# Slice attention: the second half of an image beside the first half of the next, written out, and transposes for products with the identity

## What is computed

```
h = x @ W0 + b0
sw = jax.nn.softmax(h @ Ws + bs, axis=-1)          # 16 slices a token
qkv = (h @ Wqkv + bqkv)                            # 8 heads of 32
denom = jnp.sum(sw, axis=1)[:, None, :, None] + 1e-09
qs = jnp.einsum('bhnd,bns->bhsd', q, sw) / denom   # ks, vs likewise
attn = jax.nn.softmax(jnp.einsum('bhsd,bhtd->bhst', qs, ks) / scale, axis=-1)
tok = jnp.einsum('bhst,bhtd->bhsd', attn, vs)
out = jnp.einsum('bhsd,bns->bnhd', tok, sw).reshape(b, n, H * D)
return out @ Wout + bout                           # added to x
```

## Time and profile before

| | |
|---|---|
| median of three runs | 10232.95 us (10220.48, 10232.95 and 10233.31) |
| the profiled execution's own time | 10221.47 us |
| its span in the trace | 10219.7 us |
| busy over the span | PE 8073.3 us (79%), DVE 7633.6 (75%), POOL 6829.2 (67%), ACT 5138.6 (50%) |
| slice attention in the span | from about 9430 to 9728 us |

### The profile page before, as it was taken

One profiled execution on the slowest core, in us unless ns is written; L12 is line 12 of the kernel. 1 busy time (PEld: TensorE's weight loads), 2 busy tenths in 40 slices (PEclk: granted clock), 3 DMA queues, 4 the chain that ended last, 5 costly groups with the idle time before them and its releaser, 6 DMA issues. The chain is left out here.

```text
span 10219.7 us, 112146 instructions
## 1 busy us (share of the span) xinstructions
PE 8073.3 (79%) x34375; PEld 3937.8 (39%) x34375; DVE 7633.6 (75%) x6810; ACT 5138.6 (50%) x6133; POOL 6829.2 (67%) x3866
## 2 busy tenths in 40 slices
PE   0158888888888888888888879799749999985769
PEld 0123333333333333333333333233237777753522
DVE  8769999999999999999999953477735655534144
ACT  0046666666666666666666623367615554421123
POOL 0059999999999999999999963300067777761047
PEclk9679999999999999999999988699969999965579
DMA  0057677677767766666676740000032222210022
GB/s 10 0 138 182 175 179 180 178 178 177 180 175 178 181 177 177 180 177 177 177 181 175 178 87 1 11 1 1 1 35 29 27 29 27 27 17 5 0 71 89
DMA packets 385896, 1064.96 MB, mean 104 GB/s; under 512 B 106434, under 2 KB 129602, under 8 KB 383378
## 3 DMA queue, kind: packets, MB, share of 16 engines
q1 hardware_dynamic: 338482, 1044.16, 39.8%
q0 software_dynamic: 47136, 17.04, 3.8%
HBM read 995.98 MB, written 63.50 MB: 104 GB/s over the span
## 5 line engine op out<-in xcount | busy, mean ns | idle before, releaser
L535 POOL TENSOR_TENSOR hC<-h,Cb 128x1024 f32<-128x1024 f32 x1536 | 3600.9, 2357 | 434.6 <-DVE h L630 413.7
L630 DVE TENSOR_TENSOR_SCAN h<-dA,B_ps 128x1024 f32<-128x1024 f32 x1344 | 3073.1, 2287 | 156.4
L308 PE MATMUL y_ps<-hC,con 128*128 128x512 f32 x6144 | 2969.9, 606 | 80.5 <-DVE gz L636 80.3
L455 ACT ACTIVATE dA<-delta,negA 128x1024 f32<-128x1024 f32 x1344 | 1535.3, 1145 | 1204.6 <-DVE h L630 1200.3
L616 DVE TENSOR_TENSOR B_ps<-dx,B_ps 128x1024 f32<-128x1024 f32 x1344 | 1623.9, 1208 | 166.3 <-PE B_ps L302 166.3
L308 PEld LDWEIGHTS y_ps<-hC,con 128*128 128x128 f32 x6144 | 1186.2, 194 | 1145.5 <-issue 943.2
L2626 POOL DMA_INDIRECT g_got<-scratch_node,g_idx x1152 | 1143.6, 993 | 359.8 <-issue 350.7
L302 PE MATMUL B_ps<-Bpart,sel 96*128 96x512 bf16 x2688 | 828.6, 390 | 648.0 <-DVE h L630 645.7
L2676 PE MATMUL g_pick<-g_third,g_hot 128*128 128x256 bf16 x10752 | 1260.9, 274 | 0.0
L2676 PEld LDWEIGHTS g_pick<-g_third,g_hot 128*128 128x128 bf16 x10752 | 1020.2, 98 | 203.8 <-issue 81.9
L2722 ACT ACTIVATE g_hot<-g_fill 128x512 bf16<-128x512 f32 x896 | 485.8, 594 | 653.2 <-PE g_fill L2659 651.5
(11 more groups left out here) (493 smaller groups left out, 11652.4 us busy)
## 6 DMA issues: line engine op xcount, KB each, us to landing
Cb<-scratch_c_rows SPq DMA_DIRECT2D x3072, 256.0 KB, 4.1
drive<-scratch_c_rows SPq DMA_DIRECT2D x384, 256.0 KB, 5.2
eb_share<-scratch_gate_rows SPq DMA_DIRECT2D x128, 256.0 KB, 3.5
scratch_c_rows<-BCrow SPq DMA_DIRECT2D x96, 256.0 KB, 4.0
scratch_edge<-g_out SPq DMA_DIRECT2D x64, 384.0 KB, 2.3
par<-in_ssm SPq DMA_DIRECT2D x48, 395.5 KB, 5.3
g_got<-scratch_node,g_idx POOLq DMA_INDIRECT x1152
scratch_place<-s_zero SPq DMA_DIRECT2D x4, 1024.0 KB, 11.1
```

The costliest lines, as they stand in the source:

```text
L308: last = nc.tensor.matmul(y_ps[:, hs], con[:, K_ID:K_ID + P], hC[k % DEEP][:, hs], start=(k == 0), stop=(k == STEPS - 1))
L455: A(dA[k % DEEP][:, :], delta[d][:, :], ACT.Exp, scale=negA[:, n:n + 1]).then_inc(decay_ready, 1)
L535: G.tensor_tensor(hC[k % DEEP][:, :], hst[k % DEEP][:, :], Cb[k % DEEP][:, :], ALU.mult).then_inc(prod_ready, 1)
L630: V.tensor_tensor_scan(hst[k % DEEP][:, ::step], decayed[:, ::step], driven[:, ::step], 0.0, ALU.mult, ALU.add).then_inc(scanned, 1)
```

## The change

In `slice_attn_stage` the hardware loops are replaced by a Python loop that writes every image out. Each turn of it holds the second half of image `img` ("old") and the first half of image `img + 1` ("new"), interleaved group by group on each engine; there are nine turns, the first with only a first half and the last with only a second half. Each half has its own three semaphores. To let the halves coexist, `swT` has two buffers; the results of `attnT`, `v` and `fold` go to other columns or banks of PSUM (`psS`, `psO`, `psQ`). The copy `tw` is gone: `turn` reads `tn_sb` itself, and `turn` and `swT` are `nc.tensor.transpose` in place of a product with the identity. The two memsets of POOL count in `loaded`. Outside the stage, `EndSearch` counts its two POOL operations in one semaphore `made`, `ad0` is cleared by DVE and not by POOL, and the late store counts in `loaded`.

```diff
--- before.py
+++ after.py
@@ -1838,9 +1838,19 @@
     ALU, ACT, AX = mybir.AluOpType, mybir.ActivationFunctionType, mybir.AxisListType.X
     BLK = range(PER)
     HG = 4
-    pe_s = Steps("turn hT h logits swT pool poolT qk v scores attnT tokT fold out")
-    act_s = Steps("copy tnT hTc esw swTc poolTc qkc eat attnTc foldc")
-    dve_s = Steps("hx lg max sub sum rsum sw dn rdn pooled vc qdiag smax ssub ssum srec attn tokm tok outb t")
+
+
+    pe_a = Steps("turn hT h logits swT pool")
+    act_a = Steps("tnT hTc esw swTc")
+    dve_a = Steps("hx lg max sub sum rsum sw dn rdn pooled")
+
+
+    pe_b = Steps("poolT qk v scores attnT tokT fold out")
+    act_b = Steps("poolTc qkc eat attnTc foldc")
+    dve_b = Steps("vc qdiag smax ssub ssum srec attn tokm tok outb t")
+
+    def count(steps, name, img):
+        return steps.after(name, img) - 1
...
-        tw = sb("tw", [P, PER, C])
-        swT = sb("swT", [SLICES, L])
+        swT = [sb(f"swT{k}", [SLICES, L]) for k in range(2)]
...
-        loaded, ones_set = sem("loaded"), sem("ones")
-        pe_done, act_done, dve_done = sem("pe"), sem("act"), sem("dve")
+        ATT, FOLD = 2 * SLICES, 2 * HG * SLICES
+        loaded = sem("loaded")
+        pe_a_done, act_a_done, dve_a_done = sem("pe_a"), sem("act_a"), sem("dve_a")
+        pe_b_done, act_b_done, dve_b_done = sem("pe_b"), sem("act_b"), sem("dve_b")
...
-                nc.gpsimd.memset(hx[:, :, :], 1.0).then_inc(ones_set, 1)
-                nc.gpsimd.memset(at[:, :, :], 0.0).then_inc(ones_set, 1)
+                nc.gpsimd.memset(hx[:, :, :], 1.0).then_inc(loaded, 16)
+                nc.gpsimd.memset(at[:, :, :], 0.0).then_inc(loaded, 16)
...
-                with pe.Fori(0, B) as img:
...
-                    act("copy")
-                    for i in BLK:
-                        last = M(psM[0:C, i * P:(i + 1) * P], tw[:, i, :], ID, start=True, stop=True)
-                    done(last)
...
+                pe.wait_ge(loaded, 64)
+                for img in range(-1, B):
+                    new, old = img + 1 < B, img >= 0
+                    if old:
+                        dve_first("pooled", img)
+                        M(psS[0:C + 1, 0:SLICES], pooled[:, :], con[0:SLICES, K_ID:K_ID + SLICES], start=True, stop=True
+                          ).then_inc(pe_b_done, 1)
+                    if new:
+                        if old:
+                            act_first("swTc", img)
+                        for i in BLK:
+                            last = nc.tensor.transpose(psM[0:C, i * P:(i + 1) * P], tn_sb[:, (img + 1) * PER + i, :], ID)
+                        last.then_inc(pe_a_done, 1)
+                    if old:
+                        act_last("poolTc", img)
+                        for j in range(4):
+                            last = M(psQ[:, j * SLICES:(j + 1) * SLICES], w[0:C + 1, SW_QKV + j * P:SW_QKV + (j + 1) * P], poolT[:, :],
+                                     start=True, stop=True)
+                        last.then_inc(pe_b_done, 1)
+                        if img >= 1:
+                            dve_last("outb", img - 1)
+                        M(psO[0:SLICES, 0:HD3], poolT[:, :], w[0:C + 1, SW_QKV + 2 * HD3:SW_QKV + 3 * HD3],
+                          start=True, stop=True).then_inc(pe_b_done, 1)
+                    if new:
+                        act_first("tnT", img + 1)
+                        for hs in halves:
+                            last = M(psM[:, hs], w[0:C, SW_0:SW_0 + P], tnT[:, hs], start=True, stop=True)
+                        last.then_inc(pe_a_done, 1)
+                        if old:
+                            dve_first("hx", img)
+                        for i in BLK:
+                            last = M(psH[:, i * C:(i + 1) * C], tnT[:, i * P:(i + 1) * P], w[0:C, SW_0:SW_0 + C],
+                                     start=True, stop=True)
+                        last.then_inc(pe_a_done, 1)
+                    if old:
+                        dve_last("qdiag", img)
+                        for g in range(2):
+                            last = M(psS[0:HG * SLICES, g * SLICES:(g + 1) * SLICES], qd[:, g, :, :].rearrange("p h s -> p (h s)"),
+                                     qk[:, 2 + g, :], start=True, stop=True)
+                        last.then_inc(pe_b_done, 1)
+                    if new:
+                        act_first("hTc", img + 1)
+                        for i in BLK:
+                            last = M(psL[:, i * SLICES:(i + 1) * SLICES], hT[:, i * P:(i + 1) * P], w[0:C, SW_S:SW_S + SLICES],
+                                     start=True, stop=True)
+                        last.then_inc(pe_a_done, 1)
+                    if old:
+                        dve_last("attn", img)
+                        for g in range(2):
+                            last = M(psS[0:SLICES, ATT + g * HG * SLICES:ATT + (g + 1) * HG * SLICES], at[:, g, :],
+                                     con[:, K_ID:K_ID + HG * SLICES], start=True, stop=True)
+                        last.then_inc(pe_b_done, 1)
+                    if new:
+                        dve_first("sw", img + 1)
+                        for i in BLK:
+                            last = nc.tensor.transpose(psM[0:SLICES, i * P:(i + 1) * P], sw[:, i, :], ID)
+                        last.then_inc(pe_a_done, 1)
+                        for i in BLK:
+                            last = M(psG[0:SLICES, 0:C + 1], sw[:, i, :], hx[:, i, :], start=i == 0, stop=i == PER - 1)
+                        last.then_inc(pe_a_done, 1)
+                    if old:
+                        act_last("attnTc", img)
+                        for g in range(2):
+                            last = M(psQ[:, g * HG * SLICES:(g + 1) * HG * SLICES], v[:, g * P:(g + 1) * P],
+                                     atT[:, g * HG * SLICES:(g + 1) * HG * SLICES], start=True, stop=True)
+                        last.then_inc(pe_b_done, 1)
+                        dve_last("tok", img)
+                        for g in range(2):
+                            last = M(psQ[0:SLICES, FOLD:FOLD + C], tok[:, g, :], w[:, SW_OUT + g * C:SW_OUT + (g + 1) * C],
+                                     start=g == 0, stop=g == 1)
+                        last.then_inc(pe_b_done, 1)
+                        act_last("foldc", img)
+                        for i in BLK:
+                            last = M(psO[:, i * C:(i + 1) * C], swT[img % 2][:, i * P:(i + 1) * P], fold[:, :], start=True, stop=True)
+                        last.then_inc(pe_b_done, 1)
...
-                    act.wait_ge(dve_done, dve_s.all(img))
-                    A(tw[:, :, :], tn_sb[:, bass.ds(img * PER, PER), :], ACT.Copy).then_inc(act_done, 1)
...
+                    if old:
+                        pe_last("v", img)
+                        final(V.tensor_copy(v[:, :], psO[0:SLICES, 0:HD3]))
+                        dve.wait_ge(act_b_done, count(act_b, "qkc", img))
+                        final(V.tensor_tensor(qd[:, :, :, :], qk[:, 0:2, :].unsqueeze(2).broadcast_to([P, 2, HG, SLICES]), mask, ALU.mult))
+                    if new:
+                        pe_first("h", img + 1)
+                        first(V.tensor_tensor(hx[:, :, 0:C], psH[:, :].rearrange("p (i c) -> p i c", i=PER),
+                                              row(w[:, SR_B0:SR_B0 + C], [P, PER, C]), ALU.add))
+                    if old:
+                        pe_last("scores", img)
+                        final(V.reduce_max(rs[:, 0, :], sc, AX))
+                        own_last("smax", img)
+                        final(V.tensor_tensor(at4, sc, rs[:, 0, :].unsqueeze(2).broadcast_to(wide2), ALU.subtract))
+                    if new:
+                        pe_first("logits", img + 1)
+                        first(V.tensor_tensor(sw[:, :, :], psL[:, 0:PER * SLICES].rearrange("p (i s) -> p i s", i=PER),
+                                              row(w[:, SR_BS:SR_BS + SLICES], [P, PER, SLICES]), ALU.add))
+                        own_first("lg", img + 1)
+                        first(V.reduce_max(r8[:, 0, :], sw[:, :, :], AX))
+                        own_first("max", img + 1)
+                        first(V.tensor_tensor(sw[:, :, :], sw[:, :, :], r8[:, 0, :].unsqueeze(2).broadcast_to(wide), ALU.subtract))
+                    if old:
+                        dve.wait_ge(act_b_done, count(act_b, "eat", img))
+                        final(V.reduce_sum(rs[:, 1, :], at4, AX))
+                        own_last("ssum", img)
+                        final(V.reciprocal(rs[:, 1, :], rs[:, 1, :]))
+                        own_last("srec", img)
+                        final(V.tensor_tensor(at4, at4, rs[:, 1, :].unsqueeze(2).broadcast_to(wide2), ALU.mult))
+                    if new:
+                        dve.wait_ge(act_a_done, count(act_a, "esw", img + 1))
+                        first(V.reduce_sum(r8[:, 1, :], sw[:, :, :], AX))
+                        own_first("sum", img + 1)
```

(83 more changed lines are left out.)

192 lines of the change are left out of this document (39 added, 153 removed).

## The result

The changed kernel takes 10162.11 us, the median of four runs from 10148.26 to 10164.97. The kernel before has 10232.19 us, with 10220.48 to 10233.31. The ratio is 0.9931, with an interval of 0.9914 to 0.9949. The forecast was 10164 us. The profiled execution took 10164.08 us, its span 10162.3, with a granted clock of 0.91 on average.

The account below looks back on a forecast made before the run. Slice attention was taken as bound by one image's latency: 293.4 us would become 228 (seven turns of 27.6, ends 20.1 and 15.0), 65 us plus 2 for the clock, giving 10164 us; range 10135 to 10192.

Parts of the forecast that it names:

- The chain and its overlap: Slice attention: one image's latency bounds the stage; overlap can fill PE's idle time, some 82 us of the 293.
- The ends: Slice attention: first half alone takes 20.1 us, second half alone 15.0 us, besides seven full turns.
- The waits: PE in a full turn: three waits stay, logits to swT 2.3 us, tokT to fold 1.0, fold to out 0.5.
- The sum of a turn: Full turn of slice attention: PE's groups 23.8 us plus waits 3.8 make 27.6 us, PE busy 86%.
- The sign given for a turn: Slice attention, sign of being right: a turn repeats every 26.5 to 27.6 us.
- The clock: Slice attention: clock rises behind pool in about half the turns, 0 to 8 us, taken as 2 to 4.
- The whole time: Whole kernel: 10154.5 us against the profiled execution, 10166 by the median's step; 10164 us forecast.
- Do transposes raise the clock?: TensorE: yes, by the sort stage's trace; by the skill's rule the gain would be 65 us and not 67.
- A: Slice attention: denser stream holds 2.4 GHz, turn 16.3 us, gain 154 us, near 10079; full form 4%.
- B: Slice attention: waits taken as covered show, 3 to 5 us a turn; gain 30 to 44 us, 10189 to 10203; 10%.
- C: Written-out program stalls on instruction arrival, decisive from 8 us a turn; at 12 us a turn 10264; 3%.
- D: Whole kernel: no change within 0.2%, 20 us; needs a stall of 6 to 8 us a turn; 3%.

Follow-up runs that it names:

- serial_written_out: Changed kernel without its overlap: still written out with transposes, but each image's first half starts after the previous image's last addition; 10210.21 us, 0.9974, stage 274.3 us.
- the better order: Changed kernel with old softmax ahead of new on DVE, attnT and tokT ahead of swT, fold before pool; 10134.59 us with transposes, 10110.71 with products.
- the reordered kernels: Changed kernel with attnT and tokT ahead of swT and fold before pool, turn and swT as transposes or products, single or doubled; 10104.58 to 10137.32 us.
- turns_in_loop: Kernel before, still a loop, with transposes in turn and swT except each group's first block, which stays a product; 10230.64 us, 0.9996, stage 289.6 us.
- fold_mid_twice: Changed kernel with attnT and tokT ahead of swT, fold before pool, and transposes of turn and swT each issued twice; 10104.58 us, 0.9875, stage 180.4.
- fold_mid_products: Changed kernel with attnT and tokT ahead of swT, fold before pool, and products in turn and swT; 10110.71 us, 0.9881, stage 179.0.
- fold_mid: Changed kernel with old softmax ahead of new on DVE, attnT and tokT ahead of swT, fold before pool; 10134.59 us, 0.9908, stage 199.2.

## Why the prediction was right

**The chain and its overlap** held. PE's idle time in the one chain of an image was what the overlap filled: 51 us of the gain vanish when the halves run in sequence (`serial_written_out`). The ends were forecast at 20.1 and 15.0 and came out at 20.1 and 15.0.

**The waits** held nearly as summed: 2.1 for 2.3 (1.53 + 0.15 and two tails of 0.2, with attnT between), 1.0 (0.79 and the tail) and 0.5 (0.30 and the tail). None of those taken as covered shows in a row.

**The sum of a turn** was 27.6, and a turn without a rise takes 27.97. The missing 0.4 lie mostly in the tail of a group's last pass, which was put at some 0.2 us for every group. It is 0.2 behind turn, `h` and `out`, but only 0.07 behind the others: v is busy 1.04 and holds PE 0.96 (0.86 was summed), hT 3.44 (3.30), scores 0.54 (0.43), pool 1.85 (1.70), swT 1.80 (1.69), poolT 0.27 (0.2). HT shows that it hangs on what follows: its tail was 0.2 before logits and is 0.07 before scores. Together these six take 0.7 more, the first wait is 0.2 shorter, and turn and qk (1.71 and 1.66 for 1.74 and 1.70) take 0.07 less. Why the tail differs no run shows.

The sign given for a turn, a repeat every 26.5 to 27.6 us, was met by none of the seven: they take 24.2, 26.1 or 28.0, and only their mean, 26.9, lies in it.

**The clock** is the term that was mis-sized, twice over. It rose behind pool in 3 of the 7 full turns, which is the half that was assumed. But each rise is worth 27.97 - 26.14 = 1.83 us and not 1.1: pool, which was to bring 0.5 of it, stays at 1.92 in two of the three, while `out` holds PE 2.23 in place of 3.47, tokT is 0.37 and fold 0.21 shorter. The first full turn, moreover, begins at the high clock left by the first half alone and takes 24.2, 3.7 less than a slow one. Together 3.7 + 1.8 + 1.8 = 7.4 us where 2 to 4 were put. The seven turns at 0.37 more cost 2.6 of that, and so 228 - 3 was forecast and 223.5 measured. The two errors are small and of opposite sign, so the total is closer than its terms.

**The whole time** is closer still, and that is luck. Against the profiled execution 10154.5 was forecast and 10164.1 measured, because other stages added 12.5 us and the stage gave 3 more than forecast. The median of 10162.11 against a forecast of 10164 is well inside what graph attention alone varies by.

**Do transposes raise the clock?** Yes: swT issued twice as transposes has it up behind pool in all seven turns. The Trainium skill (TensorE: Matmul & The Clock Gate, Part 4: PE-mode transpose) says that the full clock does not engage in transpose mode; here, in f32, the measurement decides against it, as the prediction held by the earlier trace rows. The page's own times are for bf16, which no run here has.

**What the prediction did not see** is what the transposes do on balance. Its working gave them a gain of their own, 3.4 us a turn less in turn and swT. That term is right in the sum, since the loss by the clock (the slow `h`, a rise in half of the turns) was in the other terms. But its cause was read too kindly: set against products in the same overlap, transposes lose 8 us of the stage (20 in the better order), and in the old loop they gain nothing that can be told from no change. The change's gain is that of the overlap and of the serial parts taken from the chain.

**The rivals.** A, the clock at 2.4 GHz throughout, is excluded by the mean of 0.53; the reordered kernels show that it can be had in part (0.70). B and C did not occur: the waits are as summed, and the written-out program shows no stall in sequence or overlapped. D falls with the ratio. Of the stage, 18 us went before the overlap (292.4 to 274.3). The rows of the two kernels, from start to next start, divide them: turn and swT hold PE 26.8 us less over the 8 images, the copy's 0.8 us leaves the chain seven times, 5.6 us, and the clock takes back 14.5 (`h` and hT 9.9, pool 3.0, the rest in poolT and qk). Against `turns_in_loop` the 15.3 us are the same copy, 6.0 for the one block of each group that was still a product there, and 3.6 by the clock, which was up over qk in 6 of 8 images here and in 3 of 8 there.

## What to carry to other kernels

Where one chain hops between engines and none is saturated, work out the overlap turn by turn: what a group holds the engine, and each wait that stays; here it came within 2% of the measured turn and stage. Price every group of TensorE at both clock levels, and ask of an edit that shortens a group what the clock does in the groups behind it: here, in the loop, halved passes lost 18.0 of the 20.8 us that they saved. Waits that are left in the overlapped stream can be filled by moving a short independent chain ahead of a long one, and that may raise the clock as well (24 us for both, and 20 more with longer groups).

## What the runs showed of the hardware

- Transposes in f32 bring the clock to 2.4 GHz as products of the same number of passes do: a mean of 0.70 over the stage with each issued twice (`fold_mid_twice`), 0.71 with products (`fold_mid_products`), 0.54 with each issued once (`fold_mid`).
- In the changed kernel PE ran 15.7 us without a gap, from 9490.22 to 9505.96, at a granted clock of 0.50.
- A kernel that issues 128 useless transposes is faster than the same one without, 0.9875 against 0.9908 (intervals of 0.9858 to 0.9891 and 0.9892 to 0.9925), and the stage is 19 us shorter.
- Graph attention, whose operations are the same in all kernels here, takes from 986.1 to 1003.3 us between executions, and PE is busy 810.2 to 827.3 us in it over the same 4864 rows, with a granted clock from 0.90 to 0.88. Why is open.
